# Three of nine elementwise products per strip computed by GpSimd instead of VectorE, in a convolution and deformable convolution kernel

## The reference

```python
x = x + _L0_conv_ref(_gn(x), ...)
x = x + _L1_conv_ref(_gn(x), w_off, b_off, w_def)

offsets = _conv2d(x, w_off, b_off, 1, 1)      # 18 channels: dy, dx of 9 taps
py = row + iy + dy;  px = column + ix + dx    # per tap and pixel
val = the four neighbours of (py, px), weighted by (1 - wy)(1 - wx), (1 - wy)wx, wy(1 - wx), wy wx
out = einsum('bckhw,ock->bohw', val, w_def)
```

## Time and profile before

| what | value |
|---|---|
| runs | 1301.43, 1302.1, 1303.63 us, median 1302.1 us |
| profiled execution | 1300.54 us, span 1298.7 us |
| busy, share of the span | PE 82%, DVE 68%, ACT 52%, PE weight loads 52%, GpSimd 5% |
| strip loop | from about 770 us to the end |
| hats (L1839), whole execution | 288 operations, mean 701 ns |
| products (L1849) | 288 operations, mean 685 ns |
| distances (L1449) | 288 operations, mean 1025 ns |
| mean granted PE clock | 0.949 of full speed |

### The profile page before, as it was taken

How to read it: one execution, slowest core, us unless ns; L and a number is a source line. 1 busy time by engine, 2 the same in 40 slices (tenths; PEclk the granted TensorE clock), 3 DMA queues, 4 the chain that set the end, 5 groups by cost and what they waited for, 6 DMA issues and landing times.

```text
span 1298.7 us, 42328 instructions
## 1 busy us (share of the span) xinstructions
PE 1061.0 (82%) x17334; PEld 681.5 (52%) x17334; DVE 887.3 (68%) x1379; ACT 669.6 (52%) x901; POOL 61.9 (5%) x87
## 2 busy tenths in 40 slices
PE   0799999987593999999965867888878887888884
PEld 0234546664241454447742325777767776776764
DVE  4877762334985878751517947888878887888870
ACT  0532433112175334332113476888878887888871
POOL 0000000000051000000000350000000000000000
PEclk9999999999795999999998876999999998999998
DMA  9000022110585000202305345443433443444331
GB/s 198 1 1 2 2 94 67 42 27 4 134 202 150 1 1 2 91 6 67 67 1 123 93 142 152 137 133 112 135 117 110 122 135 102 125 128 124 114 86 36
DMA packets 96466, 109.83 MB, mean 85 GB/s; under 512 B 10127, under 2 KB 85735, under 8 KB 94616
## 3 DMA queue, kind: packets, MB, share of 16 engines
q1 hardware_dynamic: 87816, 101.73, 28.6%
q10 hardware_dynamic: 8464, 5.37, 1.9%
HBM read 74.85 MB, written 32.22 MB: 82 GB/s over the span
## 4 chain that ended last, share of the span: by engine, by line
issue 44%; PE 41%; DVE 5%; POOL 2%; ACT 2%; DMA 2%; SPq 1%; POOLq 0%; DVEq 0%; ACTq 0%
PE psum L832 22%; PE psum L901 13%; PE psum L965 3%; DMA xm<-x 2%; DVE v L1626 2%; PE psum L942 1%; SPq L529 1%; POOL offr L2003 1%; POOL offp L2007 1%; ACT xm L1377 1%; PE psum L979 1%; PE psum L923 1%; DVE xm L1792 1%; PE psum L932 1%; DVE stats L1795 1%
## 5 line engine op out<-in xcount | busy, mean ns | idle before, releaser
L832 PE MATMUL psum<-v,u 64*64 64x512 f32 x3072 | 336.8, 597 | 17.7 <-DVE v L1626 12.7
L1449 ACT ACTIVATE dist<-psum 128x1024 f32<-128x1024 f32 x288 | 288.9, 1025 | 54.1 <-PE psum L1028 39.1
L832 PEld LDWEIGHTS psum<-v,u 64*64 64x64 f32 x3072 | 148.2, 134 | 204.8 <-issue 188.1
L1839 DVE TENSOR_SCALAR dist<-dist 128x1024 f32<-128x1024 f32 x288 | 201.9, 701 | 77.1 <-ACT dist L1449 75.5
L1075 PE MATMUL psum<-hat,win 64*64 64x144 f32 x4096 | 199.5, 318 | 32.7 <-DVE outt L1875 18.2
L1849 DVE TENSOR_TENSOR hat<-dist 128x512 f32<-128x512 f32 x288 | 194.8, 685 | 0.3
L1148 PE MATMUL psum<-val,wdefs 64*64 64x256 f32 x1944 | 166.0, 395 | 33.0 <-ACT val L1452 24.1
L1075 PEld LDWEIGHTS psum<-hat,win 64*64 64x64 f32 x4096 | 152.7, 135 | 66.3 <-issue 64.7
L1452 ACT ACTIVATE val<-psum 128x864 f32<-128x864 f32 (+3 forms) x230 | 146.5, 675 | 34.6 <-PE psum L1075 22.7
L1028 PE MATMUL psum<-offs,sels 61*64 61x256 bf16 x2304 | 139.1, 284 | 21.4 <-issue 11.2
L1148 PEld LDWEIGHTS psum<-val,wdefs 64*64 64x64 f32 x1944 | 91.1, 136 | 48.1 <-issue 44.6
(11 more groups left out here) (144 smaller groups left out, 1097.2 us busy)
## 6 DMA issues: line engine op xcount, KB each, us to landing
win<-pixd SPq DMA_DIRECT2D x256, 68.0 KB
win<-pixd SPq DMA_DIRECT2D x128, 136.0 KB
raw<-x SPq DMA_DIRECT2D x16, 512.0 KB, 7.4
x1d<-xm SPq DMA_DIRECT2D x16, 512.0 KB, 6.0
pixd<-turned SPq DMA_DIRECT2D x64, 128.0 KB, 3.9
x1t<-x1d SPq DMA_DIRECT2D x63, 128.0 KB, 2.8
out<-outt SPq DMA_DIRECT2D x63, 128.0 KB, 2.6
offd<-offp SPq DMA_DIRECT2D x48, 128.0 KB
```

The costliest lines, as they stand in the source:

```text
L832: mm = pe.matmul(o, u4[half, i, v, ky, :], V[half, at:at + CHUNK, cg, v, :], start=start, stop=stop, skip_group_check=True)
L1449: act.activation(dist_at(j, n), psum[:, slot:slot + 2, :], ACT.Abs).then_inc(dist_abs, 1)
L1839: dve.tensor_scalar(d, d, 1.0, 1.0, ALU.min, ALU.subtract).then_inc(hats_made, 1)
```

## The change

GpSimd makes the products of taps 1, 4 and 7 of every strip, DVE those of the other six. Both write into the same `hat`, and count with a semaphore each. PE's group 0 waits for both counts, and ACT, before it writes a distance buffer again, for the count of the engine that made that product (`product_made`). GpSimd takes its three products of a strip in order, each after the hats of its tap, and the first of each strip from the third strip on after the sampling two strips before has ended, as DVE does ahead of its product 0. The memset of `val` stays ahead of them.

```diff
+POOL_UNITS = [1, 4, 7]
+DVE_UNITS = [0, 2, 3, 5, 6, 8]
...
+        prod_pool = sem("prod_pool")
...
+        def product_made(s, n):
+
+            if n in POOL_UNITS:
+                return prod_pool, len(POOL_UNITS) * s + (POOL_UNITS.index(n) + 1)
+            return prod_dve, len(DVE_UNITS) * s + (DVE_UNITS.index(n) + 1)
+
+        def product_of(j, n):
+
+            d = dist_at(j, n)
+            lo = TAP_PITCH * n + n % K
+            to = hat[:, j, lo:lo + BANK].rearrange("p (b n) -> p b n", b=IMAGES)
+            return to, d[:, :, 0:PS * HALF_W], d[:, :, PS * HALF_W:]
...
-                    pe.wait_ge(prod_dve, UNITS * (s + 1))
+                    pe.wait_ge(prod_dve, len(DVE_UNITS) * (s + 1))
+                    pe.wait_ge(prod_pool, len(POOL_UNITS) * (s + 1))
...
-                    act.wait_ge(prod_dve, UNITS * q + (m_ + 1))
+                    act.wait_ge(*product_made(q, m_))
...
                         hats(s + 1, 1 - j, n)
-                        if n > 0:
+                        if n - 1 in DVE_UNITS:
                             product(s + 1, 1 - j, n - 1)
...
+            def products(s, j):
+
+                for n in POOL_UNITS:
+                    if n == POOL_UNITS[0] and not (isinstance(s, int) and s < 2):
+                        pool.wait_ge(vals_made, GROUPS * (s - 1))
+                        settled(pool)
+                    pool.wait_ge(hats_made, UNITS * s + (n + 1))
+                    pool.tensor_tensor(*product_of(j, n), ALU.mult).then_inc(prod_pool, 1)
+
+            products(0, 0)
+            products(1, 1)
+            with pool.Fori(1, STRIPS // 2) as h:
+                products(2 * h, 0)
+                products(2 * h + 1, 1)
```

More of the change, by code:

```diff
@@ L1499, in edge_absolute @@
                 if e:
-                    act.wait_ge(prod_dve, UNITS * STRIPS)
+                    act.wait_ge(prod_dve, len(DVE_UNITS) * STRIPS)
+                    act.wait_ge(prod_pool, len(POOL_UNITS) * STRIPS)
                 act.activation(dist[:, DIST_RING - 1, :, 0:K * W0], psum[:, 0:2, 0:K * W0], ACT.Abs).then_inc(edge_abs, 1)
@@ L1845, in product @@
                 dve.wait_ge(hats_made, UNITS * s + (n + 1))
[L1846 to L1849, removed]
+                dve.tensor_tensor(*product_of(j, n), ALU.mult).then_inc(prod_dve, 1)
             def edge_product(e):
@@ L1906, in _ @@
                 hats(0, 0, n)
-                product(0, 0, n)
+                if n in DVE_UNITS:
+                    product(0, 0, n)
             strip_step(0, 0, 1)
```

## The result

| | before | changed |
|---|---|---|
| median | 1301.76 us (4 runs) | 1311.78 us (4 runs) |
| ratio, 95% interval | | 1.0078, 1.0056 to 1.0099 |
| profiled execution, its span | 1300.54, 1298.7 | 1312.85, 1311.0 |

The change makes the kernel 10 us slower. The time between the results of two strips tells where it went. Every second step is short and almost constant, the others are longer and vary; I call them short and long steps.

What follows compares the result with a forecast made beforehand. The prediction took a ring of waits among DVE, PE and ACT, not a full engine, to bound the strips. 27 x 0.44 = 11.9 us plus 1.0 for strips 0 and 1 gave +12.9 and a forecast of 1315, range 1300 to 1324.

Steps and rivals of the forecast that it cites:

- The ring through the result: Strip loop: waits among DVE, PE and ACT; the eight DVE operations from hats 1 to the result set the strip.
- A DVE product is stopped too, taken from the reading rate: Product against product: full wait, since a product reads 2 x 512 elements in 0.60 us, nearest to the stopped hats.
- Net 0.44 per strip: Each strip's result comes 0.44 us later: hats 2 ends 1.04 late, the missing product 1 returns 0.60.
- 27 strips at the full loss: Strip loop: 27 strips each lose 0.44 us, together 11.9 us.
- the sum: Whole kernel: 11.9 us from 27 strips and 1.0 from strips 0 and 1, together +12.9 us.
- 1.0 us for strips 0 and 1: Loop start: six products on GpSimd lose up to 2.6 us, 1.0 taken, since ACT and PE set part.
- Product 4 beside the result costs nothing, hats 5 is 0.46 late: After product 3: GpSimd's product 4 leaves the result unlengthened; hats 5 ends 0.46 us late against 0.60 saved.
- The gain of 0.35 per strip if GpSimd were free: Hats 1 to the result: without product 1, waiting for hats 3's distance, at most 0.35 us gained per strip.
- the second rival: DVE's unbroken row keeps GpSimd out until the result; DVE gains 27 x 0.35 = 9.5 us, 1293; chance 0.08.
- these eight operations: DVE's operations from hats 1 up to the result; what they gain or lose, the strip gains or loses.
- the first: Rival: GpSimd stops DVE's hats but not its products; hats 2 0.58 us late against 0.60 saved, 1303; chance 0.16.
- the third: Rival: the result is stopped as well, behind product 4, 1.06 us more per strip, 1344; chance 0.07.

Runs made afterwards that it cites:

- Tap 1 alone: The changed kernel with only product 1 on GpSimd, products 4 and 7 back on DVE: 1.0058 of the kernel before.
- taps 4 and 7: Two kernels with one product each on GpSimd, the other eight on DVE: only product 4, 1.0023 of the kernel before; only product 7, 1.0009.
- the pair test: Kernel before plus a test behind the last result, six DVE operations against one GpSimd operation: beside its product, products and hats take 4.77 us, results 3.68.
- only the result moved: The kernel before with DVE's result one position earlier in its order (RESULT_AT 5 to 4): 0.9978 of before.
- small windows: The kernel before, each load of pixel windows from the third strip on moving 64 values per place instead of 17 x 64: 0.9971 of before.
- the kernels with products left out: Kernel before, products 1, 4, 7 made by nobody from strip 2: 1.0028; with the result one position earlier 1.0005; with small window loads as well 0.9958.

## Why the prediction was right, and where it was not

**The direction and the size held**: 1315 forecast, range 1300 to 1324, measured 1311.8. As a difference 12.9 us were forecast, and the medians differ by 10.0.

*The ring through the result*: right for a delay. Tap 1 alone gives 1.0058 of 1.0078 and all of the short steps' loss; taps 4 and 7 leave the short steps as they were. As the only bound it was wrong, see below.

*A DVE product is stopped too, taken from the reading rate*: right. 1.75 beside GpSimd's product in the pair test, 1.64 in strip 0.

*Net 0.44 per strip*: measured 0.49 in the short steps. Both parts hold: 1.08 late instead of 1.04, 0.60 back. PE's wait for the result grew to 0.97 where 1.1 was foreseen.

*27 strips at the full loss*: too much. This term failed in size. The long steps lose 0.29 on average, not 0.44, while the short ones lose a little more; together 11.2 us over 29 steps where the sum had 11.9. That the two are so close is in part luck. Two causes stand in the traces: in eight of the fifteen long steps DVE already waited for ACT's distances between hats 1 and the result, so a part of the stop fell into that wait; and the two steps with the jump of PE's loop were 1.2 us shorter in the changed kernel's execution, beside a shorter stretch at the half clock. The rows of before showed one short step (14.45) and the average of all (457 us over 30 strips is 15.2), and I did not ask what made the others longer; the jumps of PE's loop are in no term.

*1.0 us for strips 0 and 1*: not to be seen. From the start of the memset to the first result it took 41.9 us before (770.69 to 812.57) and 41.4 after (771.86 to 813.24). The same stretch takes 39.5 with only the result moved and 42.0 with small windows, so one execution of each cannot tell 1 us.

*Product 4 beside the result costs nothing, hats 5 is 0.46 late*: hats 5 lasted 1.16 instead of 0.69, the result stayed at 0.68, and the copy kept its place. The kernel with tap 4 alone still lost 0.23%, which stays open.

*The gain of 0.35 per strip if GpSimd were free, and with it the price of the second rival, 1293*: wrong, and the largest error in the working, though no term of the sum. The kernel without these products measured 1.0028. I took the ring as the only bound; a path through PE's weighing, its distances and ACT is right behind it, and DVE's row from hats 1 to the result filled with waits for it. The statement that what these eight operations gain or lose, the strip gains or loses, held for the loss in the short steps and not for the gain. Even a GpSimd that disturbed nobody would have gained nothing here.

*The rivals*: the first falls by the stopped DVE products, the second by the entry at the first boundary, the third by results of 0.68 in the strips and six in 3.68.

**Open**: what makes the other thirteen long steps long. The loads account for 0.28 us of it. Twelve of the fifteen long steps before, and no short one, hold 0.27 to 0.33 us in which ACT waits for nothing that the profile shows, ahead of distance 0, at the start of a turn of ACT's loop over two strips (the earlier trace rows has one, at 1002.83). The record of the loop's jump itself lasts 0.04 to 0.06 us, and a kernel with this loop written out was not tried. Open too: the 0.23% of tap 4 alone, the 1.76 us of one long step, and why the kernels with products left out are not at least as fast as those with them.

## What to carry to other kernels

Before an elementwise operation goes from VectorE to GpSimd, set what VectorE saves (0.60 us here) against what it stands still (1.08) for each GpSimd operation that its neighbours collide with: here the products (two inputs in SBUF) and the hats (1024 elements per partition in 0.60 us) did, the results (one operand in PSUM) did not. Then ask where the stop falls; three products cost 0.78% or 0.31% by their place in the order. And a saving on the engine that others wait for is worth only the distance to the next path, which leaving the work out measures in one run.

## What was unexpected of the hardware

GpSimd does not lose against an engine that issues without a gap: its record grew by 0.3 us in the pair test (1.57 against 1.26), and it then held DVE for 1.08, with products or hats queued there. A stopped operation shows as a longer record and not as a wait, on both engines, so neither engine's list of waits names this loss. GpSimd's multiplication of 128x512 took 1.26 us alone, as the subtraction did, where the subtractions of the first half had a median of 1.17. Its record in the strips (1.66) holds a wait of about 0.5: product 1 of 1026.96 begins inside DVE's product 0, which ends at 1027.48.

The jump back of PE's loop over eight strips came with 3.2 to 3.6 us of idle PE each time, and the granted clock, 1.0 before PE stood still, fell to 0.50 for 3.4 us or 6.8; the steps with it were 2.7 to 3.8 us longer than the median long step, before and after.
